# Where the last weights are loaded, which engine writes the padding rows, and how many PSUM banks the expert tiles use

## What is computed

```python
logits = x @ gate_w                                   # x: normalized tokens, 4112 of them, 512 wide
scores = softmax(logits); topk_w, topk_idx = top_k(scores, 2)      # 8 experts
g = silu(einsum('td,edh->teh', x, w_gate)) * einsum('td,edh->teh', x, w_up)    # h = 352
routed = einsum('teh,ehd,te->td', g, w_down, comb)    # comb: the two weights of each token
shared = silu(x @ sw_gate) * (x @ sw_up) @ sw_down    # 704 wide
out = routed + shared
```

## Time and profile before

| | us |
|---|---|
| runs | 1172.41, 1167.87, 1167.35 |
| median | 1167.87 |
| profiled execution | 1168.93 |
| its span | 1167.2 |
| rounds end, first tile starts (TensorE) | 744.7, 747.26 |
| first and last down product start | 765.26, 1154.43 |
| TensorE busy / VectorE / GpSimd / ScalarE | 1069.8 / 813.3 / 381.7 / 347.5 |

### The profile page before, as it was taken

One profiled execution on the slowest core, in us unless ns is written; L12 is line 12 of the kernel. 1 busy time (PEld: TensorE's weight loads), 2 busy tenths in 40 slices (PEclk: granted clock), 3 DMA queues, 4 the chain that ended last, 5 costly groups with the idle time before them and its releaser, 6 DMA issues.

```text
span 1167.2 us, 26583 instructions
## 1 busy us (share of the span) xinstructions
PE 1069.8 (92%) x7943; PEld 699.5 (60%) x7944; DVE 813.3 (70%) x2123; ACT 347.5 (30%) x658; POOL 381.7 (33%) x352
## 2 busy tenths in 40 slices
PE   3078898999999999999999998799999999999995
PEld 3045567667776677667766765455555555555552
DVE  7976997989889888998899655444444444444443
ACT  4413432443344333443344332111111111111110
POOL 1010220222123211332023211155555655555554
PEclk8578997999999999999999998999999999999998
DMA  8343455456545555455545894689989778777875
GB/s 260 107 144 108 116 156 153 110 158 186 157 128 154 178 161 146 133 175 166 161 119 162 268 304 153 170 165 188 207 187 183 129 127 135 132 130 128 136 127 76
DMA packets 305120, 183.32 MB, mean 157 GB/s; under 512 B 256083, under 2 KB 274899, under 8 KB 302885
## 3 DMA queue, kind: packets, MB, share of 16 engines
q1 hardware_dynamic: 288308, 136.38, 46.7%
q0 software_dynamic: 15504, 36.46, 15.2%
q10 hardware_dynamic: 1248, 9.72, 2.4%
HBM read 55.36 MB, written 79.47 MB: 116 GB/s over the span
## 4 chain that ended last, share of the span: by engine, by line
PE 73%; DVE 5%; DMA 4%; issue 2%; SPq 2%; ACT 1%; POOL 1%; POOLq 1%; DVEq 0%; ACTq 0%
PE bank L996 28%; PE bank L1156 11%; PE bank L1157 10%; PE bank L1166 10%; PE bank L1071 7%; PE bank L1010 4%; DMA wexp<-w_halves 1%; DMA wexp<-x3w 1%; PE bank L1061 1%; PE bank L1075 1%; DMA x_slots<-x3w,sl 1%; DVE wexp L1370 1%; PE bank L1060 0%; PE bank L1059 0%; PE bank L1058 0%
## 5 line engine op out<-in xcount | busy, mean ns | idle before, releaser
L996 PE MATMUL bank<-wexp 128*128 128x256 f16 (+2 forms) x3252 | 407.6, 287 | 10.6 <-issue 5.8
L996 PEld LDWEIGHTS bank<-wexp 128*128 128x128 f16 x3252 | 310.4, 99 | 91.5 <-issue 16.1
L1156 PE MATMUL bank<-wexp,rows_in 128*128 x852 | 257.8, 315 | 9.6 <-issue 4.8
L1157 PE MATMUL bank<-wexp,rows_in 128*128 x852 | 257.3, 315 | 0.0
L1709 DVE SCALAR_TENSOR_TENSOR mixed<-bank,mixed 128x352 f32<-128x352 f32 x71 | 37.3, 525 | 165.3 <-ACT mixed L1327 165.3
L974 POOL DMA_INDIRECT out<-x2w,rows_in x70 | 112.0, 1599 | 113.4 <-DMA out<-x2w,rows_in 76.7
L928 POOL TENSOR_TENSOR inv<-var,power 128x4 f32<-128x4 f32 x17 | 29.2, 1717 | 363.1 <-DVE var L1552 363.1
L962 POOL TENSOR_TENSOR ex<-base,ld 128x8 f32<-128x8 f32 x71 | 120.4, 1695 | 80.7 <-DVE ld L1687 53.8
L1156 PEld LDWEIGHTS bank<-wexp,rows_in 128*128 128x128 f16 x852 | 83.6, 98 | 67.6 <-issue 25.8
L1327 ACT ACTIVATE mixed<-bank 128x352 f32<-128x352 f32 x71 | 32.9, 464 | 298.0 <-PE bank L1157 298.0
L1071 PE MATMUL bank<-wexp 128*128 128x512 f16 x495 | 113.1, 380 | 1.6 <-DVE wexp L1386 1.6
(11 more groups left out here) (285 smaller groups left out, 1272.9 us busy)
## 6 DMA issues: line engine op xcount, KB each, us to landing
w_halves<-rows_in SPq DMA_DIRECT2D x16, 704.0 KB, 4.8
wexp<-w_halves ACTq DMA_DIRECT2D x8, 1088.0 KB, 6.1
wexp<-w_halves SPq DMA_DIRECT2D x8, 1088.0 KB, 6.3
h_tok<-tokens SPq DMA_DIRECT2D x16, 512.0 KB, 2.7
mixed<-h_tok SPq DMA_DIRECT2D x32, 256.0 KB
out<-h SPq DMA_DIRECT2D x32, 256.0 KB
w_halves<-rows_in SPq DMA_DIRECT2D x16, 384.0 KB, 5.0
rows_in<-in_L_ffn_w_gate SPq DMA_DIRECT2D x16, 352.0 KB, 5.6
```

The lines of the kernel that those rows point to most:

```text
L996: last = MM(dst, stat_of(step, a), mov_of(step, b), start=(s_ == 0 and a + b == 0), stop=(s_ == len(steps) - 1 and a == 1))
L1156: MM(GB[:, 0:H], xT[b][:, a, c, :], wexp[:, u, o:o + H], start=s_, stop=e_)
L1157: last = MM(UB[:, 0:H], xT[b][:, a, c, :], wexp[:, u, o + H:o + 2 * H], start=s_, stop=e_)
```

## The change

Three edits; none changes what is computed.

1. In round 16 `first_weights(3)` (unit 7) is no longer issued between the last norm and the conversion of the down weights, but at the end of ScalarE's round, and waits for the router of chunk 16 (c_rt).
2. Padding: SP copies experts 0 to 3, ScalarE expert 4, GpSimd 5 to 7, behind its scatters of chunk 16 and with a semaphore of its own, c_zp. SP waits for c_z and c_zp before it loads tiles.
3. GB, UB and DB become pairs, used by even and odd tiles; TensorE's two waits ask for one tile less.

```diff
-        GB, UB, DB = psum[1], psum[2], psum[5]
+        GB, UB, DB = (psum[1], psum[4]), (psum[2], psum[7]), (psum[5], psum[6])
...
+        c_zp = sem("c_zp")
...
-        def pad_rows(eng, e):
+        def pad_rows(eng, e, done):
...
-                        for e in range(5):
-                            pad_rows(sp, e)
+                        for e in range(4):
+                            pad_rows(sp, e, c_z)
                         sp.wait_ge(c_wo, 32 * NCH)
-                        sp.wait_ge(c_z, 16 * E)
+                        sp.wait_ge(c_z, 16 * 5)
+                        sp.wait_ge(c_zp, 16 * (E - 5))
...
+                    if isinstance(k, int) and k == LAST:
+                        gp.wait_ge(c_ri, 1)
+                        gp.wait_ge(c_pw, 64)
+                        for e in range(5, E):
+                            pad_rows(gp, e, c_zp)
+                            apart(gp, c_sep)
...
                 def gate_up(i, b, unit):
                     pe.wait_ge(d_xl[b], xcount(i, b))
-                    at_least(pe, d_gf, i)
+                    at_least(pe, d_gf, i - 1)
...
                 def down(i, b, unit):
                     pe.wait_ge(d_tr[b % 4], turns(i, b))
-                    at_least(pe, d_ye, i)
+                    at_least(pe, d_ye, i - 1)
...
-                            pad_rows(act, 5)
+                            pad_rows(act, 4, c_z)
                         silu(n, 2)
-                        if isinstance(k, int) and k == LAST:
-                            pad_rows(act, 6)
                         ghigh(n, 1)
                         first_weights(1)
                         silu(n, 3)
-                        if isinstance(k, int) and k == LAST:
-                            pad_rows(act, 7)
                         ghigh(n, 2)
...
-                    first_weights(3)
+                    if not (isinstance(k, int) and k == NCH):
+                        first_weights(3)
...
+                    if isinstance(k, int) and k == NCH:
+                        act.wait_ge(c_rt, NCH + 1)
+                        first_weights(3)
```

More of the change, by code:

```diff
@@ L775, in vit_tower @@
         xcount = lambda i, b: (i - b) * (32 // UNROLL) + 32
-        def pad_rows(eng, e):
+        def pad_rows(eng, e, done):
             turn = eng.value_load(roti[0:1, e:e + 1], min_val=0, max_val=P - 1)
             row = eng.value_load(runi[0:1, e:e + 1], min_val=0, max_val=ZERO - P)
-            eng.dma_start(xs_d[bass.ds(row, P), :], pads_d[e].rearrange("r q w -> (r q) w")[bass.ds(turn, P), :]).then_inc(c_z, 16)
+            eng.dma_start(xs_d[bass.ds(row, P), :], pads_d[e].rearrange("r q w -> (r q) w")[bass.ds(turn, P), :]).then_inc(done, 16)
         with nc.Block() as block:
@@ L1155, in gate_up @@
                             s_, e_ = (c == 0 and a + w == 0), (c == KD - 1 and a == 1)
-                            MM(GB[:, 0:H], xT[b][:, a, c, :], wexp[:, u, o:o + H], start=s_, stop=e_)
-                            last = MM(UB[:, 0:H], xT[b][:, a, c, :], wexp[:, u, o + H:o + 2 * H], start=s_, stop=e_)
+                            MM(GB[b % 2][:, 0:H], xT[b][:, a, c, :], wexp[:, u, o:o + H], start=s_, stop=e_)
+                            last = MM(UB[b % 2][:, 0:H], xT[b][:, a, c, :], wexp[:, u, o + H:o + 2 * H], start=s_, stop=e_)
                     last.then_inc(d_gu, 1)
@@ L1165, in down @@
                             o = UG + (c * 2 + w) * (D // 2)
-                            last = MM(DB[:], gT2[b % 4][0:HK[c], a, c, :], wexp[0:HK[c], bass.ds(unit, 2), o:o + D // 2],
+                            last = MM(DB[b % 2][:], gT2[b % 4][0:HK[c], a, c, :], wexp[0:HK[c], bass.ds(unit, 2), o:o + D // 2],
                                       start=(c == 0 and a + w == 0), stop=(c == KH - 1 and a == 1))
@@ L1326, in expert @@
                     act.wait_ge(d_gu, i + 1)
-                    A(sg[:], GB[:, 0:H], ACT.Silu, scale=SXW).then_inc(d_sg, 1)
+                    A(sg[:], GB[b % 2][:, 0:H], ACT.Silu, scale=SXW).then_inc(d_sg, 1)
                     act.wait_ge(d_gf, i + 1)
@@ L1703, in out_of @@
                         at_least(v, d_ys[b % 2], halfcount(i, b) - 16)
-                    TS(sums_of(i, b), DB[:], wv[:, b % 2:b % 2 + 1], 1.0 / SW, ALU.mult, ALU.mult).then_inc(d_ye, 1)
+                    TS(sums_of(i, b), DB[b % 2][:], wv[:, b % 2:b % 2 + 1], 1.0 / SW, ALU.mult, ALU.mult).then_inc(d_ye, 1)
                 def expert(i, b):
@@ L1708, in expert @@
                     at_least(v, d_gl, i)
-                    STT(gx[:], UB[:, 0:H], SXW, sg[:], ALU.mult, ALU.mult).then_inc(d_gf, 1)
+                    STT(gx[:], UB[b % 2][:, 0:H], SXW, sg[:], ALU.mult, ALU.mult).then_inc(d_gf, 1)
                     v.wait_ge(d_gh, i + 1)
```

## The result

The changed kernel takes 1166.08 us (median of 20 runs, 1160.79 to 1170.96) where the kernel before, run beside it, takes 1168.92 (20 runs): a ratio of 0.9972, 95% interval 0.9959 to 0.9986. That is 0.28% or about 3.3 us, a third of the 9.6 us forecast, and outside the range.

The account below looks back on a forecast made before the run. TensorE alone was taken to bound the steady tile, so gains lay in its idle stretches and low clock: 2.2 + 2.4 + 0.8 - 1.0 + 1.3 + 1.5 + 1.7 + 0.7 = 9.6 us, giving 1158.3 us, range 1155.8 to 1162.5.

Parts of the forecast that it names:

- The last x3 transpose: Before the router's second half: without the load beside it, it lands in 3.0 us, not 5.2; +2.2 us.
- The clock behind the router: After the router: a gap of 1.4 us keeps the clock up; +2.4 us.
- That the clock falls all the same: Rival, behind the router: the clock still drops, 2.4 us less gain, 1160.7 us; chance 0.08.
- Padding: Padding copies before the first tile: moving three to GpSimd ends them 12.5 us behind c_ri, not 13.3; +0.8 us.
- the cost of 1.0 us: First tile: TensorE stands 3.2 us instead of 2.57, so the clock stays low longer; -1.0 us.
- The wait that was forecast: Before the first tile: TensorE done near 738.6, tile can start at 741.9, so it stands 3.2 us.
- the 4.5 us of these terms: First tiles, second banks: tile 1's wait +1.3, tile 2's gap +1.5, clock kept up there +1.7 us.
- what is next late: First tiles: tile 0's gated-row transpose lands 11.6 us after the first tile's start, needed at 13 to 14.
- given back in the tiles: Rival, tile stage: worse traffic against register loads costs 0.06 us a tile, 4 us, 1162.3 us; chance 0.07.
- the term of 0.7: Tail: both bank waits go, tile 70's down product waits for its transpose, last scatter-add earlier; +0.7 us.

Follow-up runs that it names:

- e1_weights: Kernel before, with only the load of unit 7 moved behind the router; ratio to the kernel before 0.9986.
- e8_reuse_regs: e4 with TensorE keeping the weight unit in a register for the first 8 tiles, two register loads a tile instead of three; ratio to the kernel before 0.9935.
- e3_banks: Kernel before, with only the second set of banks added; ratio to the kernel before 0.9985.
- e9_sp3_pool3: e8_reuse_regs with padding copies SP 3, ScalarE 2, GpSimd 3, and 12 unread products in the tail wait; ratio to the kernel before 0.9933.
- e7_stores_later: e4 with the last two stores of h moved on SP behind tile 0's transpose and the following load of rows; ratio to the kernel before 0.9977.
- e6: Changed kernel plus two extra 264 KB copies on ScalarE's queue into an unread tensor; one run, padding stretch 13.24 us.
- e5: Kernel before, with the loads of units 8 to 15 moved to later tiles as in e4; ratio to the kernel before 0.9990.
- e12: e10 with each later weight-unit load moved ahead of the load of rows on SP; ratio to the kernel before 0.9910.
- e10: As e9_sp3_pool3, but padding copies SP 4, ScalarE 2, GpSimd 2; ratio to the kernel before 0.9910.
- e2: Kernel before, with only the padding edit: SP four copies, ScalarE one, GpSimd three; ratio to the kernel before 0.9997.
- e4: Changed kernel with the loads of units 8 to 15 moved on SP from tiles 1, 4, ... 22 to 4, 7, ... 23; ratio to the kernel before 0.9925.
- e11_units_on_act: Changed kernel with the loads of units 8 to 15 issued by ScalarE behind its silu instead of by SP; ratio to the kernel before 1.0020.

## Why the prediction was wrong, point by point

**The last x3 transpose: right.** It landed in 3.0 us, and the gap fell to 1.46 us where 1.4 was said. With the same 3.4 us of low clock the stretch to c_ri is 18.3 to 18.6 us without the edit and 16.6 to 16.7 with it: 1.8 us, where 2.2 stood in the sum. The difference is that before's landing of 5.2 us was the longest of its kind, and the other executions of the old order have gaps of 3.4 to 3.5 rather than 3.6 us.

**The clock behind the router: the first term that failed, +2.4.** I compared the gap with one stall of 1.31 us that had left the clock up. The clock fell in 8 of the 10 traces with the edit, for 3.4 us, and stayed up in e1_weights and e8_reuse_regs, after the same gap. Low or not is worth 1.5 us (16.7 against 15.2). What failed is the comparison itself, the step that takes the length of the gap as what decides. Before the first tile the clock stayed up in e3_banks and e9_sp3_pool3 behind gaps of 2.35 and 2.27 us, where 2.57 in before and 2.17 in e1_weights brought it down. And the 6.8 us of before were themselves the bad case: the three other kernels without the edit show 3.4. So the term is 0 at most times and 1.5 at some. That the clock falls all the same had a chance of 0.08 and needed one of 0.8.

**Padding: right in the parts, wrong in the end, +0.8.** GpSimd's third copy was issued 8.24 us behind c_ri (8.3 was the early end of what I said). But I let it land 3.1 to 5.1 us later and took a middle value; it took the long end, 5.13. SP's fourth copy, which I had landing 11.3 to 13.3 us behind c_ri and did not count further, took the long end too, 13.20: with three copies of GpSimd's beside it its landing went from 3.76 us in before to 5.18. So GpSimd's copy by itself held SP up for only 0.17 us. The stretch is 13.2 to 13.5 us in ten of the eleven traces with the arrangement of before or after, and 12.8 in one (e7_stores_later). The experiments set the size of the error but do not prove its mechanism: the total of bytes doesn't do it (e6). What fits is how long the last copy has others beside it. It lands in 3.0 to 3.4 us where they are through 1.6 to 2.5 us after its issue (before, e1, e3, e5, e12), in 4.5 and 4.7 where they take 4.0 to 4.1 us (e9, e10), and in 5.1 to 5.3 where two are issued together at the end (after, e2, e4). No run varied this alone, so it is not shown.

**The first tile: the cost of 1.0 us was not there.** TensorE stood 4.27 us, more than the 3.2 forecast, and the clock was low for 3.4 us, as before. A longer wait did not lengthen it here. In the fourteen traces TensorE stood 1.3 to 4.3 us before the first tile, and the clock was low for 3.4 us in nine, for 6.8 us in one (e2_pads, behind 3.63 us) and not at all in four (behind 1.34, 1.40, 2.27 and 2.35 us). The wait that was forecast has a slip of its own: 744.7 less 4.6 and 1.3 is 738.8, not 738.6, and the wait 3.1 us, which changes nothing.

**The banks: right up to the first down product.** Tile 1's 1.31 us went, tile 2's gap fell from 2.47 to 0.54, and the clock stayed up. Counted from the first gate and up product, the first down product came after 13.0 us and not 18.0, which is even more than the 4.5 us of these terms. The step that failed is the sentence on what is next late. I named tile 0's transpose and found it in time, which it was, by 0.2 us (it landed at 759.74, and the down product started at 759.93). I did not follow SP's queue to tile 2. From 742.0 to the load of unit 8 at 765.92 SP has no pause over 0.5 us in after; in before it has one right behind that load, from 766.1 to 767.6, where it waits for tile 2's gated rows. So at tile 2 SP waits for the other engines in before, and they wait for SP in after. SP cannot serve an earlier TensorE, and behind that load the transpose is another 8 us on its way. e3_banks, e4_late_units and e5_before_late show the three sides of this: the banks alone keep nothing, later units give 2.1 us back, and without the second banks they give nothing. The sizes rest on one trace each, and three traces with the same tile code (before, e1_weights, e2_pads) differ by up to 3.2 us in that stretch; what is sure is the wait at tile 2, which is there in after, e3_banks and e6_more_bytes (2.0 to 2.5 us) and in no kernel without the load there or with one set of banks. My rival "given back in the tiles" had this outcome, but with a price of 0.06 us a tile over the whole stage and a chance of 0.07. It was 4.8 us in three tiles; from tile 3 on the two kernels run alike within 0.6 us.

**The tail: the term of 0.7 is right in this trace, and not in most.** The last scatter-add came 0.8 us earlier. But I priced the wait for tile 70's transpose only by its length. It is 2.0 us and more, and in 4 of 7 traces it brought the clock down, and the last scatter-add then comes 1.1 to 2.1 us later than with the clock up. This is a cost that the change adds: the two waits that it replaces, 1.45 and 1.13 us in before, did not do so in any of the four traces with one set of banks.

**The whole.** 1.8 for the router, up to 1.5 for its clock, nothing for padding and tiles, and in the tail between 0.8 gained and 1.3 lost: 0.5 to 4 us, and 3.3 measured, with an interval of 1.6 to 4.8. The three parts measured alone multiply to a ratio of 0.9968 against 0.9972 together; each of the three has an interval that holds 1, so this fits and proves nothing. Two things made the forecast too large. The 4.5 us of the banks were counted without the queue that takes them back. And the range was built from terms that all came out of one trace, of which two (a landing of 5.2 us, a low clock of 6.8) were the worst of their kind.

Open is why the set-up takes about 96.2 us in six of the fourteen traces and 99 to 100.4 in the others. It hides in every single time, and the ratios of e4_late_units and of those built on it may hold some of it: their traces have the short set-up in e4, e7, e8 and e9 and the long one in e10 and e12.

## What to carry to other kernels

When a wait is taken away at the seam of two stages, follow the queue of the engine that feeds the stage, instruction by instruction, as far as the gain is to reach, and look for the first large transfer in it: it can be harmless only because the consumer was late. A term that rests on one landing or one low clock of one trace is worth its typical value, which the other rows of its kind tell. And where a gap is shortened but not closed, the clock may go down as before; with twelve matmuls that nobody reads in a wait of 2 us it stayed up in three traces of three, without them in three of seven.

## What the runs showed of the hardware

A bulk load and a DMA transpose in two queues can hold each other up far more than by their bytes. The transfers of e11_units_on_act from 751 to 767 us (GB/s in 40 slices of 0.4 us, then by queue: packets, MB, share of the engines):

```profile
GB/s 41 133 184 201 218 247 179 189 107 70 173 143 96 116 180 244 120 92 88 33 47 27 25 29 52 35 49 48 49 49 56 248 186 192 174 174 348 44 187 269
...
q1 hardware_dynamic: 2188, 0.94, 57.9%
q10 hardware_dynamic: 144, 1.11, 44.5%
```

Both were under way all the time, and yet for some 5 us the core moved 25 to 56 GB/s, where it has 88 to 244 in the 2 us ahead of them and 174 to 348 in the 2 us behind. The load that took 6.4 us in SP's own queue, ahead of the transpose, took 15.5 here. It is one load of eight, and one queue does not rule such a case out: in e10_sp4_pool2 a transpose right behind the load took 11.2 us. The Trainium skill, DMA: Bandwidth & Descriptors, section "Issuing engines are not separate DMA queues", says that DMAs of several engines end up on the same 16 engines, so that another issuer saves only its sequencer's time. The trace agrees with it, and shows a loss besides, which that section does not speak of.

The clock answered the same gap in two ways: after 1.46 us it stayed up in two traces of ten and was low for 3.4 us in eight. Before the first tile it stayed up behind 2.35 us in one trace and was low behind 2.17 us in another.
